# A decoder layer with a state-space scan: the sum over states moved from TensorE to accumulating DMAs, four PSUM banks of scan input, and one GpSimd product per state

## The reference, cut to what matters

```
def step(state, xs):
    d_t, B_t, C_t, u_t = xs
    dA = jnp.exp(d_t[..., None] * A)
    state = state * dA + (d_t * u_t)[..., None] * B_t[:, None, :]
    y_t = jnp.einsum('ben,bn->be', state, C_t)
    return (state, y_t)
...
y = y + D[None, :, None] * u
```

## Time and profile before

| | |
|---|---|
| time, median of 3 runs | 1203.17 us (1201.85 to 1208.17) |
| the profiled execution | 1202.71 us |
| its span in the profile | 1200.8 us |
| stage 1's loop, first scan to 710 us | 640.2 us |
| busy share of the span | PE 85%, PEld 55%, DVE 72%, ACT 58%, POOL 54% |

### The profile page before, as it was taken

The page is one execution under the profiler, slowest core; times in us unless marked ns, Lnnn a source line. Parts: engine busy times, 40 slices in busy tenths (PEclk is TensorE's granted clock), DMA queues, the critical chain, the costliest instruction groups (busy, mean ns, idle before and its releaser), DMA issues. The chain is left out here.

```text
span 1200.8 us, 12841 instructions
## 1 busy us (share of the span) xinstructions
PE 1017.1 (85%) x4000; PEld 663.3 (55%) x4000; DVE 870.3 (72%) x1283; ACT 701.1 (58%) x1050; POOL 647.2 (54%) x519
## 2 busy tenths in 40 slices
PE   6776989779998689998599964659999999989998
PEld 3244444445444345444355432547877877778886
DVE  3676588859688568688789665775999999925543
ACT  3482775546775457775389515655877777624322
POOL 0458777946686946697879545432555455400000
PEclk9788999979999889999799986788999999989999
DMA  6201002022002030000041028211111111012321
GB/s 218 67 14 35 28 26 62 27 79 88 28 20 64 22 122 27 28 27 28 20 146 51 20 72 313 97 66 40 45 44 35 52 44 44 26 55 85 106 70 61
DMA packets 46450, 75.20 MB, mean 63 GB/s; under 512 B 4080, under 2 KB 12400, under 8 KB 46400
## 3 DMA queue, kind: packets, MB, share of 16 engines
q1 hardware_dynamic: 44496, 71.72, 18.6%
q10 hardware_dynamic: 1904, 2.87, 0.7%
HBM read 54.78 MB, written 19.79 MB: 62 GB/s over the span
## 5 line engine op out<-in xcount | busy, mean ns | idle before, releaser
L867 POOL TENSOR_TENSOR state<-state,crep 128x512 f32<-128x512 f32 x256 | 354.5, 1394 | 176.8 <-DVE state L706 172.3
L706 DVE TENSOR_TENSOR_SCAN state<-decay,banks 128x512 f32<-128x512 f32 x256 | 308.0, 1213 | 146.5 <-PE banks L375 137.8
L384 PE MATMUL banks<-state,ident 128*128 128x512 f32 x512 | 276.4, 623 | 4.9 <-POOL state L867 4.9
L1098 PE MATMUL banks<-x2T,wgu 128*128 128x512 f32 x1056 | 251.0, 400 | 9.0 <-POOL wgu L1403 9.0
L1098 PEld LDWEIGHTS banks<-x2T,wgu 128*128 128x128 f32 x1056 | 203.4, 193 | 55.9 <-issue 12.8
L375 PEld LDWEIGHTS banks<-ident,scaled 128*128 128x128 f32 x1024 | 131.2, 146 | 181.8 <-issue 115.1
L502 ACT ACTIVATE decay<-delta,negA 128x512 f32<-128x512 f32 x256 | 169.3, 712 | 60.6 <-DVE state L706 60.5
L491 ACT ACTIVATE scaled<-duT,BT 128x512 f32<-128x512 f32 x256 | 163.5, 710 | 52.9 <-PE banks L375 52.7
L375 PE MATMUL banks<-ident,scaled 128*128 128x128 f32 x1024 | 161.8, 283 | 31.6 <-DVE state L706 28.0
L1186 ACT ACTIVATE leaf<-bit,table,table_gap 128x512 f32<-128x512 int32 x198 | 149.5, 807 | 17.4 <-DVE w L1280 17.3
L1280 DVE COPY_PREDICATED leaf<-bits,leaf 128x512 f32<-128x512 int32 x132 | 120.2, 926 | 15.2 <-issue 13.8
(11 more groups left out here) (115 smaller groups left out, 1283.9 us busy)
## 6 DMA issues: line engine op xcount, KB each, us to landing
crep<-c_scratch SPq DMA_DIRECT2D x64, 256.0 KB, 3.2
idx_sb<-in_idx SPq DMA_DIRECT2D x33, 256.0 KB, 2.8
xT_sb<-in_xT SPq DMA_DIRECT2D x16, 256.0 KB, 4.3
x_sb<-in_x SPq DMA_DIRECT2D x4, 1024.0 KB, 4.6
x_scratch<-x_sb SPq DMA_DIRECT2D x4, 1024.0 KB, 4.4
y_scratch<-u SPq DMA_DIRECT2D x4, 1024.0 KB, 4.7
hT<-x_scratch SPq DMA_DIRECT2D x4, 1024.0 KB, 12.3
hT<-y_scratch SPq DMA_DIRECT2D x4, 1024.0 KB, 13.4
```

Source lines behind the costliest of these rows:

```text
L384: mm(banks[:, 4 + et, :], ident[:], state[:, k % ST_RING, :], start=n == 0, stop=n == DS - 1)\
L706: V.tensor_tensor_scan(state[:, k % ST_RING, :], decay[:, k % DR_RING, :], banks[:, k % 2, :], 0.0, ALU.mult, ALU.add).then_inc(scan_ready, 1)
L867: G.tensor_tensor(state[:, k % ST_RING, :], state[:, k % ST_RING, :], crep[:, g % CR, :], ALU.mult)\
L1098: last = mm(banks[:, 2 * tb + w, :], wgu[:, par, w, ws, t * P:(t + 1) * P], x2T[:, xs, t, tb * 512:(tb + 1) * 512], start=t == 0 and n == ...
```

## The change

The sum over the states leaves PE and PSUM. `add_to_sum` and `skip_add` are gone. Per group, POOL multiplies all four tiles by C in one 128x2048 instruction and issues a DMA that adds the 1 MB tile to a total in DRAM. Even states add to `y_scratch`, odd ones to a second total, `y2_scratch`; each add waits for the one two groups before. `y_scratch` starts as D u (`skip_term` on ACT, stored by SP), `y2_scratch` as the product of state 1 (stored by SP). At the end of a batch one more accumulating DMA adds the second total to the first. The ring `state` has four whole groups, and `scan` waits for the add of the group four before. The freed banks give the scan input four banks (`NB`) and PE's jobs four. `decay` shrinks from six units to four, `u` loses its second buffer, `attT` shares the memory of `q`. The sums of weighted values leave POOL: `attention_transposed` accumulates the products in PSUM instead. B, C and dt are copied out of PSUM in one instruction. The hand-written order of the other work is laid out anew.

```diff
-DR_RING = 6
-ST_RING = 6
+DR_RING = 4
+GR = 4
+NB = 4
...
+    y2_scratch = nc.dram_tensor("y2_scratch", [S, DI, L], f32, kind="Internal").ap()
...
-        PV = ([(3, j) for j in range(4)] + [(3, "half"), (3, "sum")] + [(2, j) for j in range(3)]
-              + [(2, "half"), (2, "sum")] + [(1, 0), (1, 1), (1, "sum"), (0, 0)])
+        PV = [(i, j) for i in DOWN for j in range(i + 1)]
...
-        EARLY_ATT = {(2, 0): 3, (2, 2): 2, (3, 0): 1, (3, 2): 0}
-        JOBS_AT = {(0, 1): ("in", 0), (0, 3): ("in", 1), (1, 1): ("in", 2), (1, 3): ("in", 3),
-                   (2, 1): ("kv", 0), (2, 3): ("kv", 1), (3, 1): ("kv", 2), (3, 3): ("kv", 3),
-                   (4, 1): ("q", 3), (5, 1): ("xp", 0), (5, 3): ("bt", 0),
+        EARLY_ATT = {(1, 0): 3, (1, 2): 2}
+        JOBS_AT = {(0, 2): ("in", 0), (0, 3): ("in", 1), (1, 1): ("in", 2), (1, 3): ("in", 3),
+                   (2, 0): ("att", 1), (2, 1): ("kv", 0), (2, 2): ("att", 0), (2, 3): ("kv", 1),
+                   (3, 1): ("kv", 2), (3, 3): ("kv", 3),
+                   (4, 0): ("proj", 3), (4, 2): ("proj", 2), (5, 0): ("proj", 1), (5, 1): ("xp", 0),
+                   (5, 2): ("proj", 0), (5, 3): ("bt", 0),
                    (6, 0): ("dt", 0), (6, 1): ("dt", 1), (6, 3): ("dt", 2), (7, 0): ("dt", 3),
-                   (7, 2): ("q", 2), (8, 1): ("q", 1), (9, 1): ("q", 0),
-                   (10, 1): ("proj", 3), (11, 1): ("proj", 2), (12, 1): ("proj", 1), (13, 1): ("proj", 0),
-                   (13, 3): ("duT", 0), (14, 0): ("duT", 1), (14, 1): ("duT", 2), (14, 2): ("duT", 3),
-                   (15, 0): ("att", 3), (15, 1): ("att", 2), (15, 2): ("att", 1), (15, 3): ("att", 0)}
+                   (7, 2): ("q", 3), (8, 1): ("q", 2), (9, 1): ("q", 1), (9, 3): ("q", 0),
+                   (12, 2): ("duT", 0), (13, 0): ("duT", 1), (13, 2): ("duT", 2), (14, 0): ("duT", 3),
+                   (15, 2): ("att", 3)}
+        LATE_ATT = {(0, 1): 2}
...
+        def group_sum(g):
+            if g % DS == 1:
+                return odd_first, 16 * (g // DS) + 16
+            return added[g % GR], 16 * sum(i % DS != 1 for i in range(g % GR, g + 1, GR))
...
+                def store_skip(m):
+                    sp.wait_ge(skip_ready, ET * m + ET)
+                    sp.dma_start(y_scratch.rearrange("b (t p) l -> p b t l", p=P)[:, m], skip[:]).then_inc(y_init, 16)
+
+                def store_first_odd(m):
+                    sp.wait_ge(hc_ready, DS * m + 2)
+                    sp.dma_start(y2_scratch.rearrange("b (t p) l -> p b t l", p=P)[:, m],
+                                 state[:, (DS * m + 1) % GR]).then_inc(odd_first, 16)
...
                     for t in range(QT):
-                        last = nc.tensor.transpose(banks[:, bank, t * LQ:(t + 1) * LQ], q[:, s, t * P:(t + 1) * P],
-                                                   ident[:])
+                        for j in range(i + 1):
+                            last = mm(banks[:, bank, t * LQ:(t + 1) * LQ], buf[:, j, t * P:(t + 1) * P], ident[:],
+                                      start=j == 0, stop=j == i)
...
-                    if k >= 2:
-                        pe.wait_ge(scan_ready, k - 1)
+                    if k >= NB:
+                        pe.wait_ge(scan_ready, k - NB + 1)
...
-                def add_to_sum(k):
-                    b, n, et = k // UN, k // ET % DS, k % ET
-                    if n == 0 and b:
-                        pe.wait_ge(y_ready, ET * (b - 1) + et + 1)
-                    pe.wait_ge(hc_ready, k + 1)
-                    mm(banks[:, 4 + et, :], ident[:], state[:, k % ST_RING, :], start=n == 0, stop=n == DS - 1)\
-                        .then_inc(nsum_done, 1)
...
+                def skip_term(m):
+                    act.wait_ge(ln_ready, m + 1)
+                    for et in range(ET):
+                        A(skip[:, et, :], u[:, et, :], ACT.Copy, scale=skip_d(et)).then_inc(skip_ready, 1)
...
                 def scan(k):
+                    g, et = divmod(k, ET)
+                    if et == 0 and g >= GR:
+                        summed, count = group_sum(g - GR)
+                        dve.wait_ge(summed, count)
...
-            if at in ((10, 2), (11, 2), (12, 2), (13, 2)):
-                residual(b, 13 - n)
-            elif at == (15, 0):
-                variance(b)
+            if at in ((4, 2), (5, 0), (5, 2), (6, 0)):
+                residual(b, {(4, 2): 3, (5, 0): 2, (5, 2): 1, (6, 0): 0}[at])
+            elif at == (7, 0):
+                variance(b)
+            elif at == (8, 3):
+                mean_shift(b)
+            elif n == 12:
+                normalized(b, et)
...
+                def output_product(g):
+                    pool.wait_ge(crep_in[g % CR], 16 * (g // CR) + 16)
+                    pool.wait_ge(scan_ready, ET * g + ET)
+                    G.tensor_tensor(state[:, g % GR], state[:, g % GR],
+                                    crep[:, g % CR, :].unsqueeze(1).to_broadcast([P, ET, L]), ALU.mult)\
                         .then_inc(hc_ready, 1)
+
+                def add_group(g):
+                    b, n = divmod(g, DS)
+                    if n == 1:
+                        return
+                    summed, count = group_sum(g)
+                    pool.wait_ge(hc_ready, g + 1)
+                    pool.wait_ge(*(group_sum(g - 2) if n else (y_init, 16 * b + 16)))
+                    total = y2_scratch if n % 2 else y_scratch
+                    pool.dma_start(total.rearrange("b (t p) l -> p b t l", p=P)[:, b], state[:, g % GR],
+                                   accum_op=ALU.add).then_inc(summed, 16)
+
+                def add_odd_sum(b):
+                    pool.wait_ge(*group_sum(DS * b + DS - 2))
+                    pool.wait_ge(*group_sum(DS * b + DS - 1))
+                    pool.dma_start(y_scratch[b].rearrange("(t p) l -> p t l", p=P),
+                                   y2_scratch[b].rearrange("(t p) l -> p t l", p=P), accum_op=ALU.add).then_inc(y_out, 16)
...
+                            if et == ET - 1:
+                                output_product(k // ET)
+                            if et == 1 and k >= ET:
+                                add_group(k // ET - 1)
...
+                            if b and at == (4, 0):
+                                add_odd_sum(b - 1)
...
+                add_group(DS * S - 1)
+                add_odd_sum(S - 1)
```

More of the change, by code:

```diff
@@ L101, in stage1 @@
         decay = sb("decay", [P, DR_RING, L])
-        state = sb("state", [P, ST_RING, L])
+        state = sb("state", [P, GR, ET, L])
         relu = conv_in[:, :, TAPS - 1:]
         du = expneg
+        skip = conv_acc
+        b_rows, c_rows, dt_lo = bc_dt[0:DS, :], bc_dt[DS:2 * DS, :], bc_dt[2 * DS:3 * DS, :]
         conv_w = lambda et, j: ch[:, et, j:j + 1]
@@ L124, in stage1 @@
              "y_out").split()]
+        added = [sem(f"added{r}") for r in range(GR)]
         crep_in = [sem(f"crep_in{r}") for r in range(CR)]
@@ L307, in x_proj @@
                     for et in range(ET):
-                        last = mm(banks[0:3 * DS, bank, :], xp_w[:, et, :], u[:, m % 2, et, :],
+                        last = mm(banks[0:3 * DS, bank, :], xp_w[:, et, :], u[:, et, :],
                                   start=et == 0, stop=et == ET - 1)
@@ L393, in _ @@
                         do_job(job)
-                    if k >= LAG:
-                        add_to_sum(k - LAG)
-                for k in range(UNITS - LAG, UNITS):
-                    add_to_sum(k)
             @block.scalar
@@ L475, in keep_attT @@
                 def keep_attT(c, s):
-                    if s == S - 1 and c:
-                        act.wait_ge(proj_out, S * c)
                     act.wait_ge(att_out, S * c + nth(s) + 1)
-                    A(attT[:, s].rearrange("p t l -> p (t l)"), banks[:, bank_of(("att", c, s)), :], ACT.Copy)\
+                    A(attT[:, s], banks[:, bank_of(("att", c, s)), :].rearrange("p (t l) -> p t l", l=LQ), ACT.Copy)\
                         .then_inc(attT_ready, 1)
@@ L522, in _ @@
                 act.wait_ge(setup_done, 3)
-                for et in range(S):
-                    keep_duT(0, et)
+                for lc in range(S):
+                    keep_duT(0, lc)
                 scale_input(0)
@@ L527, in _ @@
                 exp_scores(0)
+                skip_term(0)
                 for b in range(S):
@@ L553, in _ @@
                                 log_onep(m)
[L554 to L557 removed]
+                            elif n == 9:
+                                skip_term(m)
+                            elif n == 10:
+                                keep_q(c, 0)
+                        if n == 2 and b == 0:
+                            keep_attT(0, 3)
+                            keep_attT(0, 2)
+                        if n == 3:
+                            keep_attT(b, 1)
+                            if more:
+                                keep_kv(c, 1)
```

(12 more changed lines are left out.)

241 lines of the change are left out of this document (89 added, 152 removed).

## The result

| | before | after |
|---|---|---|
| time, median | 1204.70 us (4 runs, 1201.85 to 1208.17) | 1227.47 us (4 runs, 1226.92 to 1230.16) |
| profiled execution, its span | 1202.71, 1200.8 us | 1230.16, 1228.4 us |
| loop, first scan to end of last | 639.0 us (69.8 to 708.8) | 646.0 us (69.7 to 715.7) |
| end of last scan to stage 2's first load | 9.3 us | 29.1 us |

The ratio is 1.019 (95% interval 1.017 to 1.022): the change makes the kernel 23 us slower, where 42 us less were forecast. Of the 27.6 us between the two spans, 7.0 lie in the loop and 19.8 in the tail; the rest is within 1 us.

A forecast was written before the change was run, and what follows sets the result against it. The prediction took the loop to be a chain hopping between engines, then bound by VectorE: 443 + 70 + 70 = 583 us, 57 less than 640; with 15 more in the tail, 1161 us, range 1095 to 1250.

The forecast's parts named there:

- 443 (VectorE): VectorE's floor in the loop: 487 - 9 - 50 + 15 = 443 us, the 15 for gaps between scans.
- 70 (held): Time VectorE's loop steps are held at the port shared with POOL: 70 us, between 0 and 96.
- 70 (waits): Waits left in the loop: half of today's 137.8 us of scans waiting for PE, 70, between 20 and 138.
- The tail: Last scan to stage 2: a product 4.5, then issue 2 and landing 8, twice: 24.5 us, 15 more than today.
- The bound of 96 us: Most that VectorE could be held in the loop: 29 steps, each up to 3.3 us.
- The scaling from the earlier trace: Today's 33 us held without `variance`, scaled by 4.5/1.28 and by 288/354, gives 94 us.
- Rival 3: Port taken strictly: 35 one-input VectorE steps each wait out a product, 158 us; loop 671, total 1249; chance 0.13.
- My own signs: Signs of being right, among them L618 and `normalized` above their means of today, and POOL DMA issues of about 2 us.
- landing: Time for an accumulating 1 MB DMA to land: about 8 us, so neither later adds nor scans wait.
- X: POOL's time to issue one accumulating DMA: taken as 2.0 us, between 0.37 and 4.5.
- Rival 1: Slower: an issue costs POOL 4.5 us, so POOL has 679 us in the loop; total 1262; chance 0.20.
- Rival 2: PE clock falls: PE's 300 us of loop work become 530, banks late, waits 110 us, about 1200; chance 0.12.

The follow-up runs named there:

- e6_before_product: Kernel before with the product with C as one 128x2048 instruction per state, state ring of eight, sums six units late, skip terms at n = 1: 1273.7 us.
- e5_two_banks: Changed kernel with two PSUM banks of scan input instead of four: 1220.7 us.
- e12_two_banks_ring: Changed kernel with one 128x512 product per unit behind its scan, a decay ring of six units and two banks of scan input: 1184.8 us.
- e14_unit_ring_plain: Changed kernel with one product per unit, decay ring of six, plain SP stores instead of adding DMAs, sums over states and of totals left out: 1087.4 us.
- e1_four_tiles: Changed kernel with the product with C as four 128x512 instructions in a row at the same place: 1205.3 us.
- e11_per_unit_ring: Changed kernel with one 128x512 product per unit behind its scan and a decay ring of six units: 1174.2 us.
- e4_plain: Changed kernel with POOL's adding DMAs turned into plain SP stores, the last sum left out, so nothing is summed over states: 1181.9 us.

## Why the prediction was wrong

**The sum.** It was 443 (VectorE) + 70 (held) + 70 (waits) = 583. Measured: 415.9 + 125.6 + 104.5 = 646.0. The steps that failed are the one for the port, "I take 70, because POOL runs a little behind and DVE often gets in first" (125.6, 56 us too little), and the one for the waits, "I take half of today's 137.8 us, 70" (90.0 for PE, and 14.5 for everything else, 35 too little). The adds had no term on VectorE's port at all. The floor was 27 too high, 15 of it from gaps that I added: scans directly behind one another start 1.13 us apart in the kernel before and last 1.21, so their records overlap, and busy time has no gaps to be added. The rest is 6 us more held before than I had counted, 5 more of VectorE's work that went, and 1 from the window's end at 710 us. The tail was forecast at 24.5 and took 29.1, the ramp changed by 0.1. 1161 + 63 + 5 = 1229; the profiled execution took 1230.2.

**Held time.** The bound of 96 us was itself too low. It counted one step per state of up to 3.3 us. Yet the larger steps of softplus came behind products too (L634 and L638: 23.1 us held in six instructions), and so did the softmax's. The scaling from the earlier trace rows assumed that holding grows with the length of POOL's instruction; in e6_before_product, with that edit and what it needs, 42 us held came with 18 more in waits. Rival 3 had this mechanism and took 158 us for it, 1249 in all: the 125.6 measured are nearer to it than to my 70. Its sign, "single DVE steps of 4 to 9 us all over the loop", is there: L638's mean is 6452 ns, L669's 4431. But it counted steps with one input only, and some 50 of the 125.6 us are in steps with two (L649, L654, L669, L679). My own signs, L618 and `normalized` above their means of today, both failed: 1099 against 1118 ns, and 770 against 1067. The holding fell on other steps.

**The waits.** Here the reasoning failed, not a size. Four banks were to give PE a lead of four scans; e5_two_banks shows that they gave nothing with this decay ring, and e12_two_banks_ring that they are worth 10.6 us once it is wide. The other edit in the same lines, the decay ring from six to four, was read as "ACT may lead by four scans only", priced with the banks at half of today's waits. I had not asked what stands behind the waiting decay in ACT's list: the next scaled input, and copies for PE's jobs. It cost 29.5 us. With a ring of six VectorE's idle time is 73.6 us, which is about the 70 of the forecast. That PE was to be no longer the scans' main releaser was wrong even then: 59.0 of these 73.6 us are waits for PE.

**Issue and landing.** X was taken as 2.0 us and is 1.3 by its record, 0.83 to the next start and 1.6 where products follow at once. POOL's busy time, 447.5 us, is under the 499 of the forecast. Rival 1 (the issue bounds the kernel) is out; that it too said "slower" is luck. The engines' 6.2 us per MB was 6.3; landing was 8 and is 9.9, so that adds reach the scans four states later only 5 times, for 6.2 us. By the formula of the Trainium skill ("DMA: Bandwidth & Descriptors", anatomy of one DMA) it would have been 4.4 us, an estimate; the measurement says more than twice that for an adding DMA of this shape. Beside the tail's 19.6 us the adds cost held time, 17.2 us beside the long product and 52.7 beside the short ones, and there I had priced them at nothing.

**The clock.** Rival 2's sign came exactly (0.75, with scans waiting for PE), and so did the direction of its waits: it had 110 us, idle time is 104.5. But 31 of the waits for PE went with the wider decay ring, at a granted clock of 0.77, so these did not need a faster clock to go; its share of the rest is open. Its work for PE was wrong: 300 us at full speed were to become up to 530, and it is 377.3 at 0.94 and 431.5 at 0.75.

**Was the gain there?** With the three costs off (e14_unit_ring_plain, which leaves out the sum over the states), the loop is 528.1 us, even under the 583 of the forecast. So the room is there for whoever can sum the states without POOL's DMA issues. How much of it comes from moving the sum off PE and how much from the new order is not shown: on the old kernel one piece of order alone gave 30.0 us of loop.

## What to carry to other kernels

Before a POOL instruction is made longer or a DMA is given to POOL, list VectorE's steps that may meet it and price each at one whole POOL instruction at least, and where POOL issues DMAs at its whole run of back-to-back work; fewer and longer instructions saved POOL 48 us here and cost the kernel 24 to 69. When a change pays for one ring with another's memory, ask what stands in the engine's list behind the instruction that waits on the smaller ring: that, and not the ring's own engine, is what comes late. And where a rearrangement comes with the change, try it alone on the old kernel: here moving four transposes was worth 26 us by itself.

## What the runs showed of the hardware that I had not expected

- A VectorE sum of 0.66 us took 10.50 us, across five POOL instructions (e1_four_tiles). Even the `variance` of the earlier trace rows, on 4 elements per partition, took 8.31, in a kernel in which POOL issues no DMA; another of its four took 0.17.
- Behind a DMA issue POOL's back-to-back records overlap by some 0.5 us (165.31 + 5.05 against 169.82 in e1_four_tiles), and VectorE does not get in between them: 76.1 us held in steps that waited through several instructions in e11_per_unit_ring, 10.0 in e14_unit_ring_plain.
- A scan, which has one input in PSUM, was never held in the changed kernel: shortest, median and longest of the 256 are 1187, 1206 and 1223 ns.
- A 128x2048 POOL product behind a DMA issue has a longer record, 5.00 to 5.05 us in place of 4.50, and the next issue starts 0.30 us after its end as after the others.
- An adding DMA of 1 MB takes 6.3 us of the 16 engines and lands in 9.9 us, SP's plain store of the same tile in 5.6 (e4_plain).
